# Attention transfers of a batch pair issued at four places in place of one, on one Trainium2 core

## The chip, the cores and the metric

The kernel runs on 1 core of one Trainium2 chip. The metric is the device time of one execution in microseconds (us); a time quoted for a kernel is the median of 3 runs. For the kernel before it is 909.63 us (909.2 to 911.69).

## What is computed

A transformer block on x of 32 batches x 64 tokens x 1024 features in float32:

```python
x = x + attn(cond(x, lengths, ...), Wq, Wk, Wv, Wo)   # cond: a masked long convolution over the 1024 features
x = x + ffn(cond2(x, weights, condition), W_base, gate_W, A, B)  # cond2: a 64x64 channel mix per batch; ffn: linear + top-2 LoRA experts
```

`attn` has 32 query heads of 32 features and 8 key/value heads, rotary positions, a causal mask and a softmax over 64 keys, then the output projection with `Wo`. Its result is added to x (the residual); that sum is called x1 below.

## The kernel before

Five instruction streams are written by hand, one for each engine, and they meet by semaphores only. Four stages follow each other: the convolution; the projections to queries, keys and values (with rotary positions); attention; and the FFN. Products of float32 accuracy are made of three passes over a high and a low part of each operand.

**Between the stages.** The projection stage writes queries, keys and values to DRAM (`q_dram`, `k_dram`, `v_dram`, shown in the profile as q_rows, k_rows, v_rows). Attention works on 16 pairs of batches (`NPAIR`), i = 0 to 15; a unit u = 2i + b is one batch of a pair, 32 units in all. For each pair these transfers are issued on SyncE's queue (SP) by `attention_transfers` (L1002):

- `load_q` (L985): 512 KB of queries of a pair into one of 2 buffers. It waits for `pe_s`, which counts the units whose scores TensorE has finished, so that the buffer is free.
- `load_kv` (L973): 128 KB of keys into one of 2 buffers and four times 64 KB of values into one of 4 buffers; it waits for `pe_s` and `pe_o`.
- `store_x1` (L993): the finished x1 of a pair to DRAM, 512 KB. It waits for `g_x1`, which counts the halves (512 features each) that GpSimd has added: 2 for a pair.
- `load_residual` (L997): 512 KB of x for a later pair, into one of 3 buffers.
- `load_w4` (L1225): one of 8 tiles of the FFN weights, 548 KB, tiles 0 to 3 during attention.

Pairs 0 to 3 are loaded in the stage before; pairs 4 to 15 by `attention_transfers`, in its iterations i = 1 to 12, each for pair i + 3.

**The steps of TensorE in attention** (`attention_matmuls`, L1105) run over w = 2 to 33. Step w does, in this order: `values` of unit w (L1057); `scores` of unit w + 3 (L1037), which waits for `ld_q` and `ld_k` of that unit's pair; and `project` (L1101), the half n = w % 2 of the output projection of pair w // 2 - 1. So step 2i + 2 projects the first half of pair i, and step 2i + 3 begins with values of unit 2i + 3, then scores of unit 2i + 6, the first unit of pair i + 3, and then projects the second half of pair i.

**The other engines.** ScalarE copies the projection out of PSUM (`take_projection`, L1198). GpSimd runs in each of its steps w (`attention_scale`, L1178): `subtract_max` of unit w + 2 (L1128, counted by `g_sub`), `normalise` of unit w + 1 (L1142), and `add_residual` (L1176, counted by `g_x1`), which waits for ScalarE's copy. The half n = 0 of pair i is added in GpSimd's step 2i + 3; with it `g_x1` reaches 2i + 1. VectorE scales the scores (L1119), takes maxima and sums (L1124, L1136 to L1138) and transposes the probabilities (L1148).

Of the kernel before, what the change touches and what calls it, by code (L numbers as in the profile page):

```python
# [22 lines left out]
NPAIR = NB // 2  # L23
NE, RANK = 8, 8
NPROJ = NE + NE * RANK
NBASE = NPROJ + L
# [71 lines left out]
def build(nc, x_conv, x_nat, lens, cond, modes, d_skip,  # L98
          w_qk, w_v, w_o, w_cond, w_ffn, w_b, consts, out):
    ctx = ExitStack()  # L100
    with ctx:
# [3 lines left out]
        def signal(name):  # L105
            return ctx.enter_context(nc.semaphore(name))

        def signals(name, ring):
            return [signal(f"{name}{i}") for i in range(ring)]
# [69 lines left out]
        def take(stack, name, shape, dt=F32):  # L179
            used.setdefault(stack, []).append(int(np.prod(shape[1:])))  # L180
            return sb(name, shape, dt, stack)
# [25 lines left out]
        def spare(name, part, j, shape):  # L207
# [33 lines left out]
        WB_FREE = 4  # L241
# [11 lines left out]
        wb_raw = [take(s5, f"wb_raw_{t}", [P, 2, NBASE]) for t in range(WB_FREE)]  # L253
# [14 lines left out]
        ld_w4, ld_p4 = signals("ld_w4", NJ), signal("ld_p4")  # L268
# [19 lines left out]
        pe_s, v_sc, v_max, g_sub, a_exp, v_sum, v_rec, g_prob = [signal(n) for n in (  # L288
            "pe_s", "v_sc", "v_max", "g_sub", "a_exp", "v_sum", "v_rec", "g_prob")]
        v_pt, pe_o, a_othi, v_otlo, pe_y, a_pr, g_x1 = [signal(n) for n in (  # L290
            "v_pt", "pe_o", "a_othi", "v_otlo", "pe_y", "a_pr", "g_x1")]
# [681 lines left out]
        def load_kv(sp, i):  # L973
            if i >= 2:
                sp.wait_ge(pe_s, 2 * (i - 2) + 2)
            if i >= VR:
                sp.wait_ge(pe_o, 2 * (i - VR) + 2)
            sp.dma_start(kc[:, i % 2, :, :], k_dram[:, :, i * P:(i + 1) * P].rearrange("t p k -> p t k")).then_inc(ld_k[i % 2], 16)
            for quad in range(4):
                G = quad // 2  # L980
                keys = v_dram[G, :, i * P:(i + 1) * P].rearrange("(g k) c -> k g c", g=4)
                sp.dma_start(vc[quad * HB:(quad + 1) * HB, i % VR, :, :, :].rearrange("p g a d -> p g (a d)"),
                             keys).then_inc(ld_v[i % VR], 16)

        def load_q(sp, i):  # L985
            if i >= 2:
                sp.wait_ge(pe_s, 2 * (i - 2) + 2)
            sp.dma_start(q_sb[i % 2][:], q_dram[2 * i:2 * i + 2].rearrange("b p t s -> p b t s")).then_inc(ld_q[i % 2], 16)
# [4 lines left out]
        def store_x1(sp, i):  # L993
            sp.wait_ge(g_x1, 2 * i + 2)
            sp.dma_start(x1_dram[i * P:(i + 1) * P, :], xr[i % 3][:]).then_inc(st_x1[i % 3], 16)

        def load_residual(sp, i):  # L997
            if i >= 3:
                sp.wait_ge(st_x1[(i - 3) % 3], 16 * ((i - 3) // 3 + 1))
            sp.dma_start(xr[i % 3][:], x_nat[i * P:(i + 1) * P, :]).then_inc(ld_x[i % 3], 16)  # L1000

        def attention_transfers(sp):  # L1002
            for i in range(NPAIR):
                if 1 <= i < NPAIR - 3:
                    load_kv(sp, i + 3)
                    load_q(sp, i + 3)
                if i in (6, 8, 10, 12):
                    load_w4(sp, (i - 6) // 2)
                if i == NPAIR - 1:
                    load_x1(sp, 0)  # L1010
                    load_x1(sp, 1)
                    sp.wait_ge(pe_o, NUNIT)
                    for t in range(WB_FREE, WB_EARLY):
                        load_w4(sp, t)
                if i >= 1:
                    store_x1(sp, i - 1)
                    if i + 1 < NPAIR:
                        load_residual(sp, i + 1)
            sp.wait_ge(pe_y, 2 * NPAIR - 1)
            load_w4(sp, 6)  # L1020
            sp.wait_ge(st_x1[(NPAIR - 2) % 3], 16 * ((NPAIR - 2) // 3 + 1))
            load_w4(sp, 7)
            store_x1(sp, NPAIR - 1)
# [176 lines left out]
        def attention_hi(act):  # L1200
            for w in STEPS:
                if w > FIRST:
                    take_projection(act, (w - 1) // 2 - 1, (w - 1) % 2)
                if w < NUNIT:
                    o_hi(act, w)
                if w + 2 < NUNIT:
                    exponentials(act, w + 2)
                for t in W4_TILES.get(w, ()):
                    w4_hi(act, t)
                if w == NUNIT:  # L1210
                    xf_hi(act, 0)
            take_projection(act, NPAIR - 1, 1)

        def load_x1(sp, i):
            if i >= 4:
                sp.wait_ge(st_out[(i - 4) % 4], 16 * ((i - 4) // 4 + 1))
            if i >= NPAIR - 3:
                sp.wait_ge(st_x1[i % 3], 16 * (i // 3 + 1))
            sp.dma_start(x1[i % 4][:], x1_dram[i * P:(i + 1) * P, :]).then_inc(ld_x1[i % 4], 16)

        def w4_place(t, part):

            return part if t < WB_EARLY else 1 - part

        def load_w4(sp, t):  # L1225
            sp.dma_start(wb_raw[t][:, w4_place(t, 1), :], w_ffn[:, t, :]).then_inc(ld_w4[t], 16)

        def ffn_transfers(sp):
            sp.wait_ge(pe_y, 2 * NPAIR)
# [111 lines left out]
                act.activation(xf_batch(i, 0, b), mixed(b), ACT.Copy).then_inc(a_xfhi, 1)  # L1341

        def w4_hi(act, t):
            act.wait_ge(ld_w4[t], 16)
            act.activation(wb[t][:, w4_place(t, 0), :], wb_raw[t][:, w4_place(t, 1), :], ACT.Copy).then_inc(a_w4, 1)

        def w4_lo(v, t):
# [4 lines left out]
        def ffn_hi(act):  # L1352
            act.wait_ge(pe_y, 2 * NPAIR)
            for t in range(WB_EARLY, NJ):
                w4_hi(act, t)
            act.wait_ge(ld_p4, 16 * 2)
            act.activation(bexp_hi[:], bexp_raw[:], ACT.Copy).then_inc(a_p4, 1)
            for i in range(NPAIR + 1):
                if i >= 1:
                    act.wait_ge(v_gate, GATE_STEPS * (i - 1) + 2)  # L1360
                    act.activation(gt[:, 0, :], joint_bank(i - 1, 0)[:, 0:NE], ACT.Exp, bias=gs[:, 1:2],
                                               accum_out=gs[:, 2:3]).then_inc(a_gate, 1)
                    if i > 0:
                        act.wait_ge(pe_ht, i)
                    if 3 * (i - 1) > 0:
                        act.wait_ge(pe_out, 3 * (i - 1))
                    act.activation(ht[:], turned_h(i - 1), ACT.Copy).then_inc(a_hthi, 1)
                if i + 1 < NPAIR:
                    xf_hi(act, i + 1)
# [78 lines left out]
        @block.sync  # L1448
        def _(sp):
            load_parameters(sp)  # L1450
            conv_loads(sp)
            qkv_transfers(sp)
            attention_transfers(sp)
            ffn_transfers(sp)
# [80 lines left out]
```

## Time and profile before

| | before |
|---|---|
| median of 3 runs | 909.63 us (909.2 to 911.69) |
| the profiled execution's own time | 913.52 us |
| its span, first to last instruction | 911.4 us |
| TensorE (PE) busy | 880.3 us, 97% |
| VectorE / ScalarE / GpSimd busy | 444.2 / 202.4 / 395.4 us |
| mean granted TensorE clock | 0.999 |
| DMA | 105.35 MB, mean 116 GB/s |

The rows below come from this one execution. A timeline row gives start, duration, engine, source line, operation, output<-input, shape and count, and in brackets the idle time of that engine just before with what ended it. SPq is SyncE's queue: the duration there is that of issuing a transfer, not of the transfer. A clock of 1.00 is 2.4 GHz, 0.50 is 1.2 GHz. Source lines are those of the kernel before.

### The profile page before, as it was taken

What the parts mean: (1) busy time and instruction counts of PE and PEld (TensorE: products, weight loads), DVE (VectorE), ACT (ScalarE), POOL (GpSimd) and SP (SyncE); (2) the same over time, 40 slices, a digit from 0 to 9 for tenths busy, and PEclk for the clock granted to TensorE, in tenths of its full rate; (3) what the DMA queues carried; (4) which work ended last, traced back from release to release, by engine and by line L of the source; (5) the groups of instructions that cost most, each with busy time, mean ns of one, the idle gap of its engine ahead of it and who ended that gap; (6) DMA issues with size and microseconds to landing.
All of it is one profiled execution on the core that took longest, in us unless ns stands there. A gap on an engine that the chain in (4) does not pass through costs nothing.

```text
span 911.4 us, 24899 instructions
## 1 busy us (share of the span) xinstructions
PE 880.3 (97%) x11054; PEld 766.0 (84%) x11054; DVE 444.2 (49%) x931; ACT 202.4 (22%) x365; POOL 395.4 (43%) x294
## 2 busy tenths in 40 slices
PE   2999999999999999999999999999999999999997
PEld 2888899988888888888777777777789999999997
DVE  6656562111222222259887767788533443334444
ACT  4435652100000000023122222233321101011010
POOL 1344465302555556569978878777511000000000
PEclk9999999999999999999999999999999999999999
DMA  2797787311223222256545464543352121222201
GB/s 68 181 212 198 182 192 184 99 58 58 81 70 103 72 69 74 54 174 171 148 137 158 129 169 149 173 140 108 127 179 88 57 93 57 85 72 69 92 26 69
DMA packets 82090, 105.35 MB, mean 116 GB/s; under 512 B 41536, under 2 KB 54464, under 8 KB 81984
## 3 DMA queue, kind: packets, MB, share of 16 engines
q1 hardware_dynamic: 81472, 103.24, 39.7%
q8 instruction: 87, 1.43, 0.7%
q0 software_dynamic: 512, 0.53, 0.2%
q14 instruction: 19, 0.16, 0.1%
HBM read 74.08 MB, written 29.65 MB: 114 GB/s over the span
## 4 chain that ended last, share of the span: by engine, by line
PE 90%; DMA 5%; DVE 2%; SPq 1%; issue 1%; ACT 0%; DVEq 0%
PE ps L835 24%; PE ps L1287 21%; PE ps L1101 20%; PE ps L541 7%; PE ps L799 5%; PE ps L552 3%; PE ps L1057 3%; PE ps L1037 3%; DMA kpad<-ksb 2%; PE ps L1260 2%; DMA xc<-in_dram 1%; PE ps L1307 1%; DMA toep<-kpad 1%; PE ps L1308 1%; SPq L512 1%
## 5 line engine op out<-in xcount | busy, mean ns | idle before, releaser
L1287 PE MATMUL ps<-wb,xf 128*128 128x420 f32 (+1 forms) x1152 | 195.2, 329 | 0.0
L1287 PEld LDWEIGHTS ps<-wb,xf 128*128 128x128 f32 x1152 | 189.5, 188 | 2.9 <-issue 0.2
L835 PE MATMUL ps<-y_hi,w_hi 128*128 128x512 f32 x320 | 125.1, 391 | 0.0
L835 PE MATMUL ps<-y_hi,w_lo 128*128 128x512 f32 x320 | 124.5, 389 | 0.0
L835 PE MATMUL ps<-y_lo,w_hi 128*128 128x512 f32 x320 | 124.5, 389 | 0.0
L1101 PE MATMUL ps<-y_hi 128*128 128x512 f32 x256 | 103.1, 403 | 0.2
L541 PE MATMUL ps<-xc,toep 64*128 64x192 f32 (+4 forms) x1088 | 97.7, 330 | 4.3 <-DMA xc<-in_dram 2.9
L1101 PE MATMUL ps<-y_hi,y_lo 128*128 128x512 f32 x256 | 100.2, 392 | 1.2 <-issue 1.2
L1101 PE MATMUL ps<-y_lo,y_hi 128*128 128x512 f32 x256 | 100.1, 391 | 0.0
L541 PEld LDWEIGHTS ps<-xc,toep 64*128 64x128 f32 x1088 | 89.9, 187 | 8.3 <-DMA xc<-in_dram 3.3
L942 POOL TENSOR_TENSOR rot<-rot,cst 128x512 f32<-128x512 f32 x40 | 52.7, 1318 | 72.8 <-DVE rot L913 72.8
L1142 POOL TENSOR_TENSOR sc<-sc,stat 128x1024 f32<-128x1024 f32 x32 | 65.7, 2052 | 33.3 <-DVE stat L1138 33.3
L835 PEld LDWEIGHTS ps<-y_hi,w_hi 128*128 128x128 f32 x320 | 60.1, 188 | 12.6
L835 PEld LDWEIGHTS ps<-y_hi,w_lo 128*128 128x128 f32 x320 | 60.1, 188 | 12.6
L835 PEld LDWEIGHTS ps<-y_lo,w_hi 128*128 128x128 f32 x320 | 60.1, 188 | 12.3
L913 DVE LOAD_MASK_SELECT rot<-ps x40 | 0.6, 14 | 141.0 <-PE ps L835 141.0
L1128 POOL TENSOR_TENSOR sc<-sc,stat 128x1024 f32<-128x1024 f32 x32 | 61.2, 1912 | 9.4 <-DVE stat L1124 8.9
L664 POOL TENSOR_TENSOR y_lo<-ym,y_hi 128x256 fp32r<-128x256 f32 x32 | 29.8, 931 | 78.7 <-ACT y_hi L655 78.6
L1119 DVE SCALAR_TENSOR_TENSOR sc<-ps,causal 128x1024 f32<-128x1024 f32 x32 | 39.1, 1223 | 41.3 <-PE ps L1037 41.2
L1101 PEld LDWEIGHTS ps<-y_hi 128*128 128x128 f32 x256 | 48.0, 188 | 12.7 <-issue 1.2
L1101 PEld LDWEIGHTS ps<-y_hi,y_lo 128*128 128x128 f32 x256 | 48.0, 188 | 11.8 <-issue 1.7
L625 DVE TENSOR_TENSOR ym<-ps,valid 128x512 f32<-128x512 f32 x32 | 22.1, 690 | 73.2 <-PE ps L552 55.2
(149 smaller groups left out, 1294.7 us busy)
## 6 DMA issues: line engine op xcount, KB each, us to landing
toep<-kpad SPq DMA_DIRECT2D x62, 272.0 KB, 4.8
xc<-in_dram SPq DMA_DIRECT2D x32, 256.0 KB, 5.6
q_rows<-rf SPq DMA_DIRECT2D x32, 256.0 KB, 2.6
q<-q_rows SPq DMA_DIRECT2D x16, 512.0 KB
xr<-in_dram SPq DMA_DIRECT2D x16, 512.0 KB, 4.6
x_scratch<-xr SPq DMA_DIRECT2D x16, 512.0 KB, 3.0
x<-x_scratch SPq DMA_DIRECT2D x16, 512.0 KB, 3.6
out_dram<-x SPq DMA_DIRECT2D x15, 512.0 KB, 2.6
```

Source lines behind the costliest of these rows:

```text
L541: mm = pe.matmul(ps[:, 2 * (n % 3) + r, first * NB:end * NB], toep[rows, n % TR, at:at + P], xc[rows, n // XH % XR, 1 - c, n % XH, (first ...
L552: mm = pe.matmul(ps[half * HALF:(half + 1) * HALF, 2 * (n % 3) + r, d * NB:NJ * NB], toep[rows, n % TR, at:at + HALF], xc[rows, n // XH % ...
L664: gp.tensor_tensor(y_pair(1, n, 0), ym_pair(n, 0), y_pair(0, n, 0).bitcast(F32), ALU.subtract)
L799: mm = pe.matmul(out, wv[a][:, j, h * P:(h + 1) * P], y[b][:, j, b0:b1, s0:s1], start=(j == 0 and a + b == 0), stop=(j == NJ - 1 and a == 1))
L835: mm = pe.matmul(kq_bank(n), w[a][:, j, :], yt[b][:, j, g * 512:(g + 1) * 512], start=(j == 0 and a + b == 0), stop=(j == NJ - 1 and a == 1))
L942: gp.tensor_tensor(r, r, across(C("sin"), 8), ALU.mult).then_inc(g_rsin, 1)
L1037: mm = pe.matmul(ps[G * S:(G + 1) * S, g, rep * S:(rep + 1) * S], q_sb[i % 2][rows, b, G * REP + rep, :], kc[rows, i % 2, G, b * S:(b + 1) ...
L1101: mm = pe.matmul(ps[:, 6 + n, :], heads, wo(c, t)[:, n, :], start=(at == 0), stop=(at == 3 * NQT - 1))
L1119: v.scalar_tensor_tensor(sc[:, u % CR, :].rearrange("p (g k) -> p g k", g=4), ps[:, 0:4, 0:256], INV_SQRT, across(causal[:].rearrange("p r ...
L1128: gp.tensor_tensor(sc_groups(u), sc_groups(u), along(stat[:, u % CR, 0, :], S), ALU.subtract).then_inc(g_sub, 1)
L1142: gp.tensor_tensor(sc_groups(u), sc_groups(u), along(stat[:, u % CR, 2, :], S), ALU.mult).then_inc(g_prob, 1)
L1287: mm = pe.matmul(joint_bank(i, piece)[:, 0:hi - lo], xf[i % 2][:, a, t, :], wb[t][:, w4_place(t, c), lo:hi], start=(t == 0 and a + c == 0) ...
```

## The change

In iteration i of `attention_transfers` the order and the waits are new. Before, keys and values and then queries of pair i + 3 stand first, then an FFN weight tile (at i = 6, 8, 10, 12), then the store of x1 of pair i - 1 and the residual of pair i + 1. Now the store stands first; the residual follows once `g_sub` reaches 2i + 4; queries of pair i + 3 follow once `g_x1` reaches 2i + 1; keys and values once `g_sub` reaches 2i + 5; and then half a weight tile (at i = 4 to 11). Every tile of the FFN weights, tiles 4 to 7 too, is now loaded by two transfers of half its columns, and ScalarE's `w4_hi` waits for both.

```diff
         def attention_transfers(sp):
             for i in range(NPAIR):
-                if 1 <= i < NPAIR - 3:
-                    load_kv(sp, i + 3)
-                    load_q(sp, i + 3)
-                if i in (6, 8, 10, 12):
-                    load_w4(sp, (i - 6) // 2)
                 if i == NPAIR - 1:
                     load_x1(sp, 0)
                     load_x1(sp, 1)
...
                 if i >= 1:
                     store_x1(sp, i - 1)
                     if i + 1 < NPAIR:
+                        sp.wait_ge(g_sub, 2 * i + 4)
                         load_residual(sp, i + 1)
+                    if i < NPAIR - 3:
+                        sp.wait_ge(g_x1, 2 * i + 1)
+                        load_q(sp, i + 3)
+                        sp.wait_ge(g_sub, 2 * i + 5)
+                        load_kv(sp, i + 3)
+                    if 4 <= i < 4 + 2 * WB_FREE:
+                        load_w4(sp, (i - 4) // 2, (W4_HALVES[(i - 4) % 2],))
...
-        def load_w4(sp, t):
-            sp.dma_start(wb_raw[t][:, w4_place(t, 1), :], w_ffn[:, t, :]).then_inc(ld_w4[t], 16)
+        W4_HALVES = (slice(0, NBASE // 2), slice(NBASE // 2, NBASE))
+
+        def load_w4(sp, t, halves=W4_HALVES):
+            for cols in halves:
+                sp.dma_start(wb_raw[t][:, w4_place(t, 1), cols], w_ffn[:, t, cols]).then_inc(ld_w4[t], 16)
...
         def w4_hi(act, t):
-            act.wait_ge(ld_w4[t], 16)
+            act.wait_ge(ld_w4[t], 16 * 2)
```

**SyncE's queue at the start of attention, iterations 1 and 2** (kc, vc, q: the buffers of keys, values, queries; x_scratch<-xr is the store of x1, xr<-in_dram the residual; a row's bracket names the semaphores it waits for). Before:

```order
L978 DMA kc<-k_rows 128x2x128 [waits pe_s,st_stg2,pe_o,st_stg1,st_stg0]
L982 DMA vc<-v_rows 32x4x128 x4
L988 DMA q<-q_rows 128x2x512 [waits pe_s]
L995 DMA x_scratch<-xr 128x1024 [waits g_x1]
L1000 DMA xr<-in_dram 128x1024
L978 DMA kc<-k_rows 128x2x128 [waits pe_o,pe_s]
L982 DMA vc<-v_rows 32x4x128 x4
L988 DMA q<-q_rows 128x2x512 [waits pe_s]
```

The same two iterations in the changed kernel:

```order
L995 DMA x_scratch<-xr 128x1024 [waits st_stg2,g_x1,st_stg1,st_stg0]
L1000 DMA xr<-in_dram 128x1024 [waits g_sub]
L988 DMA q<-q_rows 128x2x512 [waits pe_s,g_x1]
L978 DMA kc<-k_rows 128x2x128 [waits pe_o,pe_s,g_sub]
L982 DMA vc<-v_rows 32x4x128 x4
L995 DMA x_scratch<-xr 128x1024 [waits g_x1]
L1000 DMA xr<-in_dram 128x1024 [waits st_x10,g_sub]
L988 DMA q<-q_rows 128x2x512 [waits pe_s,g_x1]
```

The queries of pair 4 stood ahead of the first store and waited for `pe_s` alone; they now stand behind the store and the residual and wait for `g_x1` as well. The keys stand behind the queries.

**TensorE at step 3 of attention** (L1040 is `scores` and L1060 `values` in the changed kernel; nothing is moved on TensorE, and the rows read alike before but for the line numbers), the scores of unit 6:

```order
L1060 MATMUL ps<-pt,vc 32x128 [waits a_othi,v_sc,v_otlo,v_pt,ld_v1]
L1060 MATMUL ps<-pt,vc 32x128 x23
L1040 MATMUL ps<-kc,q 64x64 [waits v_sc,ld_k1,ld_q1]
L1040 MATMUL ps<-kc,q 64x64 x31
```

The first score matmul of a unit waits for the query and key transfers of its pair, and the projection of that step stands behind it. This order is unchanged; when those transfers are issued is what the change moves.

## Rows read from the trace of the kernel before

**Rows 1.** Page, part 1: busy us, share of the span, instructions.
```profile
PE 880.3 (97%) x11054; PEld 766.0 (84%) x11054; DVE 444.2 (49%) x931; ACT 202.4 (22%) x365; POOL 395.4 (43%) x294
```

**Rows 2.** Page, part 4: the chain that ended last, share by engine.
```profile
PE 90%; DMA 5%; DVE 2%; SPq 1%; issue 1%; ACT 0%; DVEq 0%
```

**Rows 3.** That chain in order of time, projections of two steps: start, us, what.
```profile
564.73 5.68 PE ps L1101 x24
572.11 5.68 PE ps L1101 x24
```

**Rows 4.** SyncE's queue, waits in 445 to 680 us: total us, times, longest.
```profile
SPq L995 <- POOL xr L1176: 163.1, 16, 15.4
```

**Rows 5.** Timeline of steps 18 and 19 (i = 8), chosen rows.
```profile
563.82 0.91 PE L1037 MATMUL ps<-kc,q 32*64 32x64 f32 x64
...
565.00 1.31 POOL L1176 TENSOR_TENSOR xr<-pr,xr 128x512 f32<-128x512 f32 x1
...
566.33 0.33 SPq L995 DMA_DIRECT2D x_scratch<-xr  x1
...
567.24 0.74 SPq L978 DMA_DIRECT2D kc<-k_rows  x1
...
570.04 0.43 SPq L988 DMA_DIRECT2D q<-q_rows  x1
...
570.34 0.94 PE L1057 MATMUL ps<-pt,vc 32*32 32x128 f32 x48
570.44 0.60 ACT L1198 ACTIVATE pr<-ps 128x512 f32<-128x512 f32 x1 [2.76 <-PE ps L1101]
570.52 1.91 POOL L1142 TENSOR_TENSOR sc<-sc,stat 128x1024 f32<-128x1024 f32 x1 [1.16 <-DVE stat L1138]
...
571.20 0.91 PE L1037 MATMUL ps<-kc,q 32*64 32x64 f32 x64
...
572.39 1.31 POOL L1176 TENSOR_TENSOR xr<-pr,xr 128x512 f32<-128x512 f32 x1
```

**Rows 6.** Page, part 6: transfers, count, KB each, median us from issue to landing.
```profile
x_scratch<-xr SPq DMA_DIRECT2D x16, 512.0 KB, 3.0
x<-x_scratch SPq DMA_DIRECT2D x16, 512.0 KB, 3.6
```

**Rows 7.** The same for 445 to 640 us: queries (no landing shown), keys, weights.
```profile
q<-q_rows SPq DMA_DIRECT2D x12, 512.0 KB
...
wb_raw<-in_dram SPq DMA_DIRECT2D x4, 548.0 KB, 6.2
kc<-k_rows SPq DMA_DIRECT2D x12, 128.0 KB, 4.8
```

**Rows 8.** The same for single key loads, issued at 451.83 us and at 567.24 us.
```profile
kc<-k_rows SPq DMA_DIRECT2D x1, 128.0 KB, 3.2
...
kc<-k_rows SPq DMA_DIRECT2D x1, 128.0 KB, 5.1
```

**Rows 9.** Windows: busy us (count) by engine, granted TensorE clock, DMA share, GB/s.
```profile
567.00:574.50 7.50, 7.50 (x139) 5.86 (x138) 5.72 (x8) 2.32 (x5) 6.18 (x5) 1.00 0.93 269
```

**Rows 10.** First matmul in the timeline; weight loads of L589 in 18:21 and 22.5:24.6 us.
```profile
17.05 1.22 PE L459 MATMUL ps<-ph 128*128 128x128 f32 x4 [17.05 <-DVE ph L450]
...
L589 PEld LDWEIGHTS ps<-cst 128*128 128x128 f32 x8 | 2.6, 336 | 0.5
...
L589 PEld LDWEIGHTS ps<-cst 128*128 128x128 f32 x6 | 1.1, 190 | 0.2
```

**Rows 11.** Windows at the end of the kernel; columns as in rows 9.
```profile
907.50:908.00 0.50, 0.14 (x1) 0.00 (x0) 0.50 (x2) 0.00 (x0) 0.00 (x0) 1.00 0.00 0
...
909.00:909.50 0.50, 0.00 (x0) 0.00 (x0) 0.00 (x0) 0.00 (x0) 0.00 (x0) 1.00 0.99 363
909.50:910.00 0.50, 0.00 (x0) 0.00 (x0) 0.00 (x0) 0.00 (x0) 0.00 (x0) 0.71 0.88 329
910.00:910.50 0.50, 0.00 (x0) 0.00 (x0) 0.00 (x0) 0.00 (x0) 0.00 (x0) 0.50 0.00 0
```

**Rows 12.** Timeline of TensorE: matmuls that an idle time of type "issue" stands before.
```profile
528.19 0.50 PE L1101 MATMUL ps<-y_hi,y_lo 128*128 128x512 f32 x1 [1.25 <-issue]
632.28 0.34 PE L1037 MATMUL ps<-kc,q 32*64 32x64 f32 x7 [0.84 <-issue]
```

**Rows 13.** Copies of FFN weights on ScalarE: duration min/median/max, first and last start.
```profile
L1345 ACT ACTIVATE wb<-wb_raw x8: 1114/1121/1132, 597.1 to 679.1; 128x1096 fp32r<-128x1096 f32 x8
```

## Prediction

> **What bounds the kernel now.** I read the page's busy times first: TensorE is busy 97% of the span, and the next engine 49% [rows 1]. Then the chain that ended last: 90% of it is TensorE [rows 2]. In attention the chain, in order of time, is a train of equal steps: one projection of 5.68 us begins 7.38 us after the last [rows 3], and the 1.7 us between are the values and the scores of the next unit. No step there waits for a transfer. So a transfer that comes earlier gains nothing, and one that comes after its first reader has need of it pushes everything behind it. SyncE's queue has time to spare: it waits 163.1 us for GpSimd's residual add ahead of the 16 stores of x1 [rows 4]. The question is thus one of due times: does each moved transfer still land before TensorE asks for it? I answer it in the timeline of one pair [rows 5], iteration i = 8, where unit 22 is the first of pair 11.
>
> **The queries and keys of pair i + 3.** TensorE asks for them at the scores of unit 2i + 6, at 571.20 us for i = 8 [rows 5]. Before, SyncE issued that pair's transfers one iteration earlier, ahead of the preceding store: what it issues at 567.24 and 570.04 us in the rows shown is already pair 12. The transfers of pair 11 had about a whole pair's time, 14.8 us, to land.
>
> Now they wait for `g_x1` to reach 2i + 1 = 17, the add of the first half of pair 8. That add cannot come before the projection of that half is done, and this projection is the last thing TensorE does in the step before the scores in question. The rows give the chain: the projection ends about 570.4; ScalarE copies it from 570.44 to 571.04; GpSimd is in `normalise` from 570.52 to 572.43, which it starts when VectorE's reciprocal is done; the add stands behind it in GpSimd's order and runs from 572.39 to 573.70 [rows 5]. So the queries are issued at about 573.72 (the store at 566.33 followed its add's end, 566.31, by 0.02 us), which is 2.5 us after TensorE wanted them on chip. The new waits on `g_sub` cost nothing: the subtraction of unit 2i + 4 (count 2i + 5) stands ahead of two adds that SyncE has by then waited for.
>
> **How late.** Issue of the queries takes 0.43 us, so the keys are issued at about 574.2 [rows 5]. The trace shows no landing for the queries. Bounds: a 512 KB transfer alone on the rings took 3.0 us (a store) and 3.6 us (a load) [rows 6]; the keys took 3.2 us where nothing stood ahead, and 5.1 us behind a store and a residual, 1 MB [rows 8], 4.8 in the median [rows 7]. Queries: 573.7 + 3.0 to 3.6 = 576.7 to 577.3. Keys: 574.2 + 3.2 to 5.1 = 577.4 to 579.3. Scores need both. Behind the queries, half of that megabyte, I take the keys halfway between alone and the median, 4.0 us: 578.2. The rings are otherwise empty by then: the store and residual issued at 566 are 1 MB, 4 us at the 269 GB/s that this stretch moved [rows 9]. So TensorE stands still from 571.2 to 578.2: **7.0 us**, with 5.5 (576.7, a query load as fast as the store, keys with it) and 8.1 (579.3) as ends.
>
> Nothing takes this up again. While TensorE waits, VectorE's next scaling waits for the same scores, and ScalarE and GpSimd wait for VectorE. The next step's chain is released by its own scores, so relative to TensorE the add of the next pair's first half comes just as late. It happens once in each of the iterations 1 to 12, the 12 query loads of the stage [rows 7]. Waits: 12 x 7.0 = 84 us.
>
> The Trainium skill speaks against the change here: "DMA: Bandwidth & Descriptors", Rules for kernel authors, advises to issue a transfer early, compute, and wait on its semaphore late. Its section Anatomy of one DMA gives about 2.0 us and the bytes over 436 GB/s for a transfer on GpSimd's path; by an estimate from it the queries would take 3.2 us, the wait would be 5.7 us, and the time 1005.6 us with the clock's term below. The sum stays with the rows' own 3.6 and 4.0.
>
> **The clock after each wait.** The one fall of the clock that the trace shows is at the end: the last matmul ends at 907.6, the granted clock is 1.00 until after 909.5 and 0.50 from 910.0 on [rows 11], level 1.2 GHz. Seven us of idle time are well past those two. What a return costs is seen at the start: after 17.05 us of idle time the first matmul begins at 17.05; weight loads of one shape took 336 ns until 21 and 190 ns from 22.5 us on [rows 10]. So some 4.0 to 5.5 us pass at half speed, and 2.0 to 2.7 us are lost. I take **2.3 us** for each wait, in the projection that follows it: 12 x 2.3 = 27.6 us. Lower end: nothing, if the clock holds.
>
> By the Trainium skill, "TensorE: Matmul & The Clock Gate", Loop structure matters more than you think, a "long DMA wait between every matmul → PE goes cold"; the end of this trace agrees with it (0.50 from 910.0 on). Without it the sum would be rival A's.
>
> **The rest costs nothing.** The store and the residual keep their place after the second add of pair i - 1; the residual's pair is not added until a pair's time later. The values land behind the keys but are read three steps later. The half weight tiles are 8 issues in place of 4 in iterations 4 to 11, and tiles 4 to 7 have 4 more; one issue is below 0.5 us, as the query's is [rows 5], on a queue with 163 us of waiting [rows 4]. Tile 0 is complete after iteration 5, before its first reader, ScalarE's copy at 597.1 us [rows 13], earlier than now, and a tile lands in 6.2 us [rows 7]. If that cover were gone, ScalarE would wait, not TensorE. What the spreading can give back are the gaps that the profile calls issue, 1.25 and 0.84 us [rows 12], should they come from crowded transfers: at most 2.1 us, taken as nothing.
>
> **The sum.** 84 + 27.6 = 111.6 us. On the profiled execution's own 913.5 us this makes 1025.1; that execution was 3.9 us above the median of the runs, so the median forecast is 909.6 + 111.6 = **1021 us**.
>
> **Rivals.**
> A. The clock holds through the waits. For it: after its first matmul TensorE never idles this long in the trace, and the only fall comes after its last. Against: 910.0 [rows 11]. Then 909.6 + 84 = 994 us.
> B. The wait is shorter: the transfers land as fast as the fastest row, and GpSimd is not held up by `normalise`. Copy and add alone would end at 571.04 + 1.31 = 572.35, and 3.0 us later the scores would start: 4.2 us of wait. With the clock's 2.3 us, 78 us: 988. Against: `normalise` is released by VectorE's reciprocal, which follows that step's scores and not the wait.
> C. The other side: the transfers are in time, and only the smoother use of the rings is left. It needs the add of a first half to end before 571.2 - 3.6 = 567.6, or the scores of unit 2i + 6 to stand a step later. The rows show 573.70, 6 us past this point, and TensorE's order stands as it was. If so, the issue gaps would go: 909.6 - 2.1 = 907.5 us, faster by 0.23%; or nothing would change.
> D. The keys come last in the crowd (5.1 us), and the clock costs 2.7 us: 12 x 10.8 = 129.6, 1039 us.
>
> **How the numbers follow.** The forecast has 0.63, A 0.16, B 0.08, D 0.10, C 0.03. The range reaches from the shortest wait of the bounds with no loss of clock, 909.6 + 12 x 5.5 = 975.6, to D, 1039. That takes in A, B and D; some 2 in 10 are left out, for C, for waits that differ from pair to pair and for sizes beyond the nearest rows. A difference under 0.3%, 2.7 us, cannot be told from none here. Slower by more than that is every case but C: 0.97; C gives 0.02 for no change and 0.01 for faster.
>
> **What would show it.** In the profile after: idle time of TensorE ahead of the score matmuls, 12 times near 7 us, ended by the key or query transfer; SyncE's query issue waiting for GpSimd's add; the pair's period up from 14.8 to about 24 us in pairs 1 to 12; the granted clock below 1.00 in that stretch alone; the other stages as long as now. The prediction is wrong if score matmuls start without such waits, if their idle times are below 5 us, or if the clock stays at 1.00.

## The result and the profile after

| | before | changed |
|---|---|---|
| median of 6 runs | 911.03 us (909.2 to 912.96) | 1019.33 us (1015.92 to 1020.9) |
| the profiled execution's own time | 913.52 us | 1020.9 us |
| its span | 911.4 us | 1018.8 us |
| TensorE busy | 880.3 us | 905.5 us |
| TensorE idle (span less busy) | 31.1 us | 113.3 us |
| mean granted clock | 0.999 | 0.945 |

The ratio is 1.1179 (95% interval 1.1158 to 1.12): 108 us slower. The forecast was 1021 us. Source lines are from here on those of the kernel that is spoken of: in the changed kernel `scores` is L1040, `project` L1104, `values` L1060, the residual add L1179, `normalise` L1145 and its copy L1201.

The page after, parts 1, 2 (the granted clock in 40 slices) and 4, which answer to [rows 1, 2]:

```profile
PE 905.5 (89%) x11054; PEld 785.4 (77%) x11054; DVE 444.8 (44%) x931; ACT 202.5 (20%) x365; POOL 395.3 (39%) x294
...
PEclk9999999999999999997777778788899999999999
...
PE 76%; DMA 7%; POOL 7%; DVE 6%; issue 3%; SPq 1%; ACT 0%; DVEq 0%; POOLq 0%
```

TensorE does the same instructions and is busy for 25.2 us longer; its share of the chain has gone from 90% to 76%, and GpSimd, VectorE and the transfers now stand in it. The clock is low in slices 19 to 29 alone, which is attention.

The waits of TensorE on the one hand, of SyncE's queue in 445 to 800 us on the other (engine, line, what it waited for: total us, times, longest):

```profile
PE ps L1040 <- DMA q<-q_rows: 87.7, 12, 8.2
```
```profile
SPq L988 <- POOL xr L1179: 88.6, 12, 8.7
```

There are 12 waits of 7.3 us in the mean, each at the first score matmul of a pair. The issue of the queries waits 12 times for the residual add, as the diff has it. The first of the twelve in the timeline, the counterpart of [rows 5]:

```profile
462.07 0.94 PE L1060 MATMUL ps<-pt,vc 32*32 32x128 f32 x48
462.29 0.26 DVE L1141 RECIPROCAL stat<-stat 128x16 f32<-128x16 f32 x1
462.63 1.90 POOL L1145 TENSOR_TENSOR sc<-sc,stat 128x1024 f32<-128x1024 f32 x1 [1.30 <-DVE stat L1141]
464.49 1.26 POOL L1179 TENSOR_TENSOR xr<-pr,xr 128x512 f32<-128x512 f32 x1
465.78 0.37 SPq L988 DMA_DIRECT2D q<-q_rows  x1
466.25 0.40 SPq L978 DMA_DIRECT2D kc<-k_rows  x1
...
470.28 1.28 PE L1040 MATMUL ps<-kc,q 32*64 32x64 f32 x64 [7.28 <-DMA q<-q_rows]
```

Read it from the end. The scores start at 470.28 after 7.28 us of idle time. The queries were issued at 465.78, 0.03 us after the add's end, and the add stood behind `normalise`, which VectorE's reciprocal released. Values ended at 463.0, so the issue came 2.8 us after the scores were due. In the next eight waits it came 2.4 us after, in the last three 3.3. The transfers of that stretch (445 to 740 us: KB each, median us to landing), for [rows 7]:

```profile
q<-q_rows SPq DMA_DIRECT2D x12, 512.0 KB, 3.9
...
kc<-k_rows SPq DMA_DIRECT2D x12, 128.0 KB, 4.1
```

The clock through that wait and behind it (columns as in [rows 9]: the third number from the end is the granted clock):

```profile
465.00:466.00 1.00, 0.00 (x0) 0.00 (x0) 0.00 (x0) 0.00 (x0) 0.75 (x1) 1.00 0.00 0
466.00:467.00 1.00, 0.00 (x0) 0.00 (x0) 0.00 (x0) 0.00 (x0) 0.00 (x0) 0.62 0.05 18
...
475.00:476.00 1.00, 1.00 (x4) 0.74 (x3) 1.00 (x2) 0.00 (x0) 1.00 (x1) 0.50 0.00 0
476.00:477.00 1.00, 1.00 (x5) 0.82 (x4) 0.99 (x1) 0.00 (x0) 0.06 (x1) 0.76 0.00 0
477.00:478.00 1.00, 1.00 (x6) 0.81 (x5) 0.25 (x1) 0.00 (x0) 0.65 (x1) 1.00 0.00 0
```

It falls to 0.50 (1.2 GHz) some 3.2 us into the idle time and is back at about 476.5, 6 us after the matmuls have begun again. In the first two us behind each of the 12 waits it is 0.50. The projection of that step shows the price, in the chain by time: 7.99 us, and 7.37 two pairs later, where a projection at the full clock took 5.68 [rows 3].

```profile
471.56 7.99 PE ps L1104 x24
...
520.67 7.37 PE ps L1104 x24
```

The FFN stage has kept its length. Windows of 233 us from its start to the end, first after, then before: the busy times agree to 0.5 us.

```profile
786.00:1019.00 233.00, 228.26 (x2219) 220.07 (x2217) 95.28 (x368) 29.08 (x81) 3.39 (x2) 1.00 0.21 73
```
```profile
679.00:912.00 233.00, 227.86 (x2216) 219.68 (x2214) 95.25 (x368) 28.66 (x81) 2.98 (x2) 1.00 0.21 73
```

So the 107.4 us between the two profiled executions are 87.7 us of waits and 25.2 us of longer matmuls, less 5.5 us: TensorE's other idle time is 25.6 us in place of 31.1. Of these 5.5 us, 3.4 lie ahead of the first wait, in the stages before attention, and 2.1 behind it. The latter is the size of the two gaps of [rows 12], 1.25 and 0.84 us, and this trace has neither.

### The profile page after: what moved, and what is told of

Same layout as the page of the kernel before. It is cut to its first block, busy times and chain, and to the rows that moved or that the text cites. A ratio compares the mean times of both kernels' runs of the same rounds, so it can differ in the third digit from the quotient of the medians.

```text
span 1018.8 us, 24933 instructions
## 1 busy us (share of the span) xinstructions
PE 905.5 (89%) x11054; PEld 785.4 (77%) x11054; DVE 444.8 (44%) x931; ACT 202.5 (20%) x365; POOL 395.3 (39%) x294
## 4 chain that ended last, share of the span: by engine, by line
PE 76%; DMA 7%; POOL 7%; DVE 6%; issue 3%; SPq 1%; ACT 0%; DVEq 0%; POOLq 0%
PE ps L835 21%; PE ps L1293 19%; PE ps L1104 12%; PE ps L541 7%; DMA q<-q_rows 5%; PE ps L799 4%; PE ps L552 3%; PE ps L1040 3%; POOL sc L1145 3%; POOL sc L1131 2%; PE ps L1266 2%; DVE sc L1122 2%; PE ps L1060 2%; DVE stat L1127 2%; POOL xr L1179 1%
## 5 line engine op out<-in xcount | busy, mean ns | idle before, releaser
L1104 PE MATMUL ps<-y_hi 128*128 128x512 f32 x256 | 112.5, 440 | 0.2 <-POOL y_lo L970 0.2
L1040 PE MATMUL ps<-kc,q 32*64 32x64 f32 x2048 | 33.6, 264 | 87.7 <-DMA q<-q_rows 87.7
L1104 PE MATMUL ps<-y_lo,y_hi 128*128 128x512 f32 x256 | 108.3, 423 | 0.0
L1104 PE MATMUL ps<-y_hi,y_lo 128*128 128x512 f32 x256 | 106.8, 417 | 0.0
L1131 POOL TENSOR_TENSOR sc<-sc,stat 128x1024 f32<-128x1024 f32 x32 | 61.0, 1907 | 113.3 <-DVE stat L1127 113.2
L1040 PEld LDWEIGHTS ps<-kc,q 32*64 32x64 f32 x2048 | 28.9, 159 | 95.0 <-DMA q<-q_rows 90.6
L1145 POOL TENSOR_TENSOR sc<-sc,stat 128x1024 f32<-128x1024 f32 x32 | 65.6, 2051 | 35.4 <-DVE stat L1141 35.4
L1104 PEld LDWEIGHTS ps<-y_hi 128*128 128x128 f32 x256 | 53.5, 209 | 14.8 <-issue 0.8
L1104 PEld LDWEIGHTS ps<-y_hi,y_lo 128*128 128x128 f32 x256 | 53.1, 207 | 12.3
```

Source lines behind the costliest of these rows:

```text
L1040: mm = pe.matmul(ps[G * S:(G + 1) * S, g, rep * S:(rep + 1) * S], q_sb[i % 2][rows, b, G * REP + rep, :], kc[rows, i % 2, G, b * S:(b + 1) ...
L1104: mm = pe.matmul(ps[:, 6 + n, :], heads, wo(c, t)[:, n, :], start=(at == 0), stop=(at == 3 * NQT - 1))
L1131: gp.tensor_tensor(sc_groups(u), sc_groups(u), along(stat[:, u % CR, 0, :], S), ALU.subtract).then_inc(g_sub, 1)
L1145: gp.tensor_tensor(sc_groups(u), sc_groups(u), along(stat[:, u % CR, 2, :], S), ALU.mult).then_inc(g_prob, 1)
```

## Experiments

The theory: everything that is lost comes from queries and keys that are issued after TensorE is due to read them, first as idle time and then as lost clock. Rivals: the new order or the other moves cost by themselves; the 20 us beyond the waits are not the clock. Runs were timed beside the kernel before on the same chip, whose medians were 912.58 us beside runs 1, 3, 4 and 5 and 911.76 us beside runs 2, 6, 7 and 8; differences below are against these.

**1. The early loads back, the rest of the change kept.**

```diff
             for i in range(NPAIR):
+                if 1 <= i < NPAIR - 3:
+                    load_kv(sp, i + 3)
+                    load_q(sp, i + 3)
...
-                    if i < NPAIR - 3:
-                        sp.wait_ge(g_x1, 2 * i + 1)
-                        load_q(sp, i + 3)
-                        sp.wait_ge(g_sub, 2 * i + 5)
-                        load_kv(sp, i + 3)
```

> Of the change this leaves the store ahead of the residual with its new wait, and the FFN weights in halves; keys, values and queries stand again at the head of the iteration, without a wait for the residual add. Theory (the whole loss is queries and keys that are issued after TensorE is due to read them): 909 to 913 us, no idle time of TensorE ahead of the score matmuls, clock 1.00. Rival (part of the loss is the other moves: the residual's wait, 8 more issues on SyncE's queue, half transfers): more than 915 us.

Measured: 913.14 us, ratio 1.0011 (0.9988 to 1.0034), clock 0.999. No wait of TensorE for queries or keys is left in the profile; ahead of one score matmul it calls 0.5 us issue, as it does 0.84 us before [rows 12]. The residual's wait, the halves of the weights and the further issues cost nothing that can be measured; all of the loss is in the five lines taken out.

**2. The same places, one pair ahead.**

```diff
-                    if i < NPAIR - 3:
-                        sp.wait_ge(g_x1, 2 * i + 1)
-                        load_q(sp, i + 3)
-                        sp.wait_ge(g_sub, 2 * i + 5)
-                        load_kv(sp, i + 3)
...
+                if i < NPAIR - 4:
+                    sp.wait_ge(g_x1, 2 * i + 1)
+                    load_q(sp, i + 4)
+                    sp.wait_ge(g_sub, 2 * i + 5)
+                    load_kv(sp, i + 4)
```

> The changed kernel with the same four places and the same new waits, but the queries, keys and values that are issued there are those of pair i + 4 instead of i + 3, so that each has a pair's time to land. Theory: no idle time ahead of the scores, the time of the kernel before within 0.3%; what the even spacing can give back on top are the issue gaps, at most 2 us. Rival (the waits or the spacing cost something by themselves, on SyncE's queue or the rings): over 0.5% slower.

Measured: 912.03 us, ratio 1.0005 (0.9991 to 1.002). With all four places and every new wait in force, the loss is gone as soon as the loads belong to the next pair; their two query and key buffers are free at that point already. And the even spacing that the change has in it gains nothing that can be measured: transfers were hidden before, and two gaps like those of [rows 12] are there still, 1.0 and 0.6 us. This is the repaired form of the change, and it does not beat the kernel before.

**3. Without the wait for the add.**

```diff
                     if i < NPAIR - 3:
-                        sp.wait_ge(g_x1, 2 * i + 1)
                         load_q(sp, i + 3)
```

> The changed kernel without the one wait of SyncE for the add of a pair's first half; the order of the transfers stays. Theory: queries and keys are then issued some 6.5 us earlier, at once behind the store and the residual, and land 1.0 to 2.5 us after the scores are due instead of 7.3; such idle times are too short for the clock to fall: 12 x 1.0 to 2.5, 921 to 940 us. Rival (the new order behind the store and residual is what costs, not the wait): near 1019 us, idle times near 7 us as in the changed kernel.

Measured: 957.77 us, ratio 1.048 (1.0441 to 1.0519). The idle times are about as expected, 1.7 to 2.7 us; the time is not. Waits of TensorE, one of the waits, and the windows around it:

```profile
PE ps L1039 <- DMA q<-q_rows: 24.9, 11, 2.7
```
```profile
563.52 1.12 PE L1039 MATMUL ps<-kc,q 32*64 32x64 f32 x45 [2.44 <-DMA q<-q_rows]
```
```profile
562.00:563.00 1.00, 0.00 (x0) 0.00 (x0) 0.00 (x0) 0.00 (x0) 1.00 (x2) 1.00 0.95 216
563.00:564.00 1.00, 0.48 (x33) 0.51 (x35) 0.00 (x0) 0.00 (x0) 0.85 (x2) 0.55 0.38 85
...
569.00:570.00 1.00, 1.00 (x4) 0.72 (x3) 1.00 (x2) 0.00 (x0) 1.00 (x1) 0.54 0.00 0
570.00:571.00 1.00, 1.00 (x6) 0.82 (x5) 1.00 (x1) 0.00 (x0) 0.08 (x1) 1.00 0.00 0
```

The clock fell here after 2 us of idle time and stayed at 0.50 for some 6.8 us, most of them beside matmuls. It fell behind 10 of the 12 waits, in five of them only after the scores had begun. TensorE is busy 902.8 us, 22.5 more than in the kernel before, nearly as much more as in the changed kernel. So of the 50 us that this execution lost (962.87 us, the slowest of the four) 27.5 are waits, and the rest is the clock; that such waits are too short for it was wrong. The end of the kernel before had hinted at it [rows 11]: there the clock fell 2.1 us after the last matmul.

**4. The wait filled with matmuls that nobody reads.**

```diff
             values(pe, u)
+            if u % 2 == 1 and 5 <= u <= 27:
+                keep_busy(pe, 14)
```

> The changed kernel with 14 matmuls that nobody reads in each of the 12 waits (6.0 us at the full clock), ahead of the score matmuls. Theory (beyond the waits of 87.7 us, the remaining 20 us are the clock's fall to 1.2 GHz in each wait): the granted clock stays at 1.00, about 1.2 us of idle time are left ahead of the scores, the scores start when they did, and the time is 999 us (996 to 1003). Rival (the 20 us are transfers beside the projection, or engines that have to start up again): 1019 us.

Measured: 999.93 us, clock 0.996. The waits that are left, in the same view as for the changed kernel:

```profile
PE ps L1040 <- DMA q<-q_rows: 13.6, 12, 1.7
```

They are 1.1 us each, beside 6 us of filling. From the end of the values to the scores the 12 waits, filling included, are 88.5 us, so the scores start about as late as in the changed kernel (87.7); yet the time is 87 us above before and not 108, and work without use has won 21 us. The clock fell twice all the same in the profiled execution, once ahead of the first wait and once behind the last. The price of the waits and that of the clock are thus apart.

**5. Only the queries late.** Keys and values are loaded at the head of the iteration, as before.

```diff
             for i in range(NPAIR):
+                if 1 <= i < NPAIR - 3:
+                    load_kv(sp, i + 3)
...
                         load_q(sp, i + 3)
-                        sp.wait_ge(g_sub, 2 * i + 5)
-                        load_kv(sp, i + 3)
```

> Of the three loads only the queries wait for the add; keys and values are early as before. Theory: the queries alone hold the scores until they land, 3.9 us after their issue, 0.4 to 0.6 us before the keys did: waits of about 6.8 us, 1012 us (1008 to 1016). Rival (the queries land last in the changed kernel, as the profile's releaser reads): no difference to 1019 us. Rival (only the keys matter): 911 us.

Measured: 1019.86 us, ratio 1.1165 (1.113 to 1.1201): no clear difference to the changed kernel, against the theory by the time alone. The waits are shorter as the theory has it, 79.3 us in place of 87.7, 6.6 us each. The chain by time shows why, here and then for the changed kernel:

```profile
473.63 4.22 DMA q<-q_rows
477.85 0.04 issue
477.90 1.29 PE ps L1040 x61
```
```profile
465.78 3.86 DMA q<-q_rows
469.64 0.64 issue
470.28 1.28 PE ps L1040 x59
```

With the keys on chip, the scores start 0.04 us after the queries land. In the changed kernel they start 0.64 us after, without a visible reason: that is the keys, which land 3.9 us after their issue at 466.25, at 470.15. Why the time does not show it can be read in two parts. TensorE is busy 912.8 us, 7.3 more than in the changed kernel. From the start of the first wait to the end (first here, then the changed kernel; length, then TensorE's busy time):

```profile
470.89:1022.80 551.91, 468.13 (x5768) 406.94 (x5768) 244.72 (x554) 95.25 (x197) 154.27 (x97) 0.89 0.27 88
```
```profile
463.00:1018.80 555.80, 463.54 (x5769) 403.99 (x5768) 244.77 (x554) 95.30 (x197) 154.40 (x97) 0.90 0.28 88
```

Of the 8.4 us that the waits are shorter, 4.6 are lost again in longer matmuls at the low clock and 3.9 are kept. These 3.9 are hidden in the profiled execution by the stages ahead of the first wait, which took 470.9 us in place of 463.0: TensorE idled 5.2 us longer there, and its clock was 0.86 in 50 to 75 us, in the convolution. The other three executions have no profile, so how much of it they share is open.

**6. Only the queries late, and the wait filled** with 14 matmuls as in 4.

> The kernel whose queries alone wait for the add, with the same 14 matmuls in each wait as in the run that kept TensorE busy in the changed kernel. Theory (the shorter wait, 6.6 us in place of 7.3, was lost again to a longer time at the low clock): with the clock held, 12 x 0.7 = 8 us less than that run, 79 us above the kernel before (75 to 83). Rival (the keys' landing is of no account): the same as that run, 87 us above it.

Measured: 988.4 us, 76.6 above before, ratio 1.0839 (1.0807 to 1.0871), against 87.4 above before and 1.0949 (1.0913 to 1.0986) in 4. With the clock held (1.0), the keys' later landing is worth 11 us by the medians. By the waits, filling included, it is 9.5 us: 79.0 us in place of the 88.5 of 4, 0.8 us a pair; the two falls of the clock in 4 are in the difference of the times too. So the theory stands, and 5 hid it, in part behind the clock. Why the clock stayed low for longer in 5 than in the changed kernel is not settled.

**7. Only keys and values late.** The queries are loaded at the head of the iteration.

```diff
             for i in range(NPAIR):
+                if 1 <= i < NPAIR - 3:
+                    load_q(sp, i + 3)
...
                         sp.wait_ge(g_x1, 2 * i + 1)
-                        load_q(sp, i + 3)
                         sp.wait_ge(g_sub, 2 * i + 5)
```

> Only keys and values wait for the add; the queries are early as before. Theory: the keys alone hold the scores; issued 0.47 us earlier than in the changed kernel, with nothing ahead of them, they land 3.2 to 3.9 us after the issue: 12 idle times of 6.0 to 6.7 us, and a loss of clock of 1.7 to 2.7 us each: 92 to 113 us above the kernel before. Rival (only the queries matter, as the profile's releaser reads): the time of the kernel before.

Measured: 991.83 us, 80 above before, ratio 1.0873 (1.0847 to 1.09). The keys alone hold the scores, so the rival is out; but the time is below the 92 to 113 us that were expected:

```profile
PE ps L1041 <- issue: 59.9, 12, 5.6
```
```profile
kc<-k_rows SPq DMA_DIRECT2D x12, 128.0 KB, 2.2
```

With nothing ahead of them the keys land in 2.2 us, where the one load of [rows 8] took 3.2; why that one was slower is open. The 12 waits are 5.0 us each, and TensorE is busy 21.6 us longer than before, so the clock's share is much as expected and the waits are short of it. The profile calls them issue: in these runs it names the queries or nothing as the releaser of this matmul, and never the keys, also where they alone were late.

**8. Without the wait for the add, and the rest of the wait filled** with 5 matmuls.

> The kernel without the wait for the add, with 5 matmuls that nobody reads (2.1 us at the full clock) in each of the 12 waits. Theory (its 45 us are waits of 2.3 us and a fall of the clock after each): the clock stays at 1.00, the scores start as late as there, and 12 x 2.3 = 28 us are left above the kernel before (24 to 32). Rival (the rest is something else than the clock): 45 us above it as without the filling.

Measured: 949.11 us, 37 above before, ratio 1.0395 (1.0366 to 1.0424): between theory and rival, and outside the 24 to 32 that were expected. The clock held (0.999), but the waits grew, since the store and with it the queries were issued later than in 3, relative to TensorE. First the step in 3 (values start at 573.25), then the same step here (values start at 565.43):

```profile
573.36 0.60 ACT L1200 ACTIVATE pr<-ps 128x512 f32<-128x512 f32 x1 [4.83 <-PE ps L1103]
574.03 1.27 POOL L1178 TENSOR_TENSOR xr<-pr,xr 128x512 f32<-128x512 f32 x1 [0.76 <-ACT pr L1200]
...
575.33 0.34 SPq L995 DMA_DIRECT2D x_scratch<-xr  x1
```
```profile
565.63 1.91 POOL L1146 TENSOR_TENSOR sc<-sc,stat 128x1024 f32<-128x1024 f32 x1 [1.29 <-DVE stat L1142]
...
567.49 1.29 POOL L1180 TENSOR_TENSOR xr<-pr,xr 128x512 f32<-128x512 f32 x1
...
568.81 0.34 SPq L995 DMA_DIRECT2D x_scratch<-xr  x1
```

In 3 the projection ran at the low clock, GpSimd was done with `normalise` before it ended, and the store went out 2.08 us after the values began. Here the projection is quick, `normalise` stands ahead of the add again, and the store goes out at 3.38 us. So it is in 7 of the 12 pairs; in the other five the store of run 3 was late as well (3.1 to 3.5 us). From the end of the values to the scores the 12 waits, filling included, are 35.6 us here and 27.5 in 3. The 8 us between them give back over a third of the clock's 22.5 us; the 37 us that are left above before are little more than the waits.

## Why the prediction was right

- **What bounds.** TensorE, and no transfer on the chain. Right: where the loads were in time, any spacing gave the same time (runs 1 and 2).
- **The due time.** Queries issued 2.5 us after the scores are due; measured 2.8 in the first wait, 2.4 in the next eight and 3.3 in the last three (i = 10 to 12, see below), 2.7 in the mean. The chain of copy, `normalise`, add and issue is the one in the rows.
- **How late.** 7.0 us foretold, 7.3 measured; 84 us, and 87.7. The keys were taken to land last, 4.0 us after issue; they landed after 3.9 to 4.3. Run 6 shows that they do land last, by some 0.8 us. That 4.0 came so close is in part luck: it was the middle between two rows, and of these the 3.2 us for keys alone is 2.2 in run 7. The queries took 3.9 us, outside the 3.0 to 3.6 that were allowed for them; the sum did not feel it, since the keys land later still. The 3.2 us estimated for the queries from the Trainium skill's figure for a transfer on GpSimd's path ("DMA: Bandwidth & Descriptors", Anatomy of one DMA) were short of the 3.9 measured on SyncE's queue.
- **The clock.** 2.3 us for each wait foretold; 25.2 / 12 = 2.1 measured, 1.7 of it in the projections behind the waits (the 12 take 6.61 to 8.08 us, 7.41 in the mean) and 0.4 in the scores (1.28 us in place of 0.91). Rival A, a clock that holds, is out: the clock was 0.50 behind every wait, and run 4 shows A's time, 87 us above before, when the clock is mostly made to hold. The Trainium skill ("TensorE: Matmul & The Clock Gate", Loop structure matters more than you think) has TensorE go cold when a long wait for a transfer stands between matmuls; this trace agrees, with 0.50 behind each of the 12 waits.
- **The rest.** Nothing foretold, nothing measured: 1.0011 with the loads early. The other side, rival C, is what run 2 made true by hand, and even then there was no gain. Rival D is out by the keys' 3.9 to 4.3 us and the clock's 2.1.
- **The sum.** 111.6 us foretold, 108.3 by the medians and 107.4 between the profiled executions: the waits took 3.7 us more than foretold, the clock 2.4 less, and 5.5 us of other idle time were not there in this execution. So the terms hold to a tenth; that the time itself came within 2 us is luck, as their errors cancel in part, and so does that of the starting point (909.6 us forecast from, 911.03 measured beside the change).

Rival B (`normalise` out of the way) did not happen in the changed kernel, but its mechanism is real: it is the 1.3 us between the stores of runs 3 and 8.

## What to carry to other kernels

Before moving a transfer behind a wait, place the wait's release and the transfer's first reader on one time line; here the release came from the very step before the reader, and the lateness could be read from the trace of before to 0.3 us in nine waits of twelve. If loads are to be spread, let them run a whole period ahead as their buffers allow; the order itself was free. And a wait on TensorE costs more than its idle time: the lost clock behind it added over a quarter here (25.2 on 87.7 us).

## What was not expected

- **The clock falls after short waits, too.** In run 3 idle times of 1.7 to 2.7 us were followed by 0.50 in 10 cases of 12, and the matmuls took 22.5 us longer, against 25.2 behind waits three times as long. Time that is won by a shorter wait can be lost again in the clock (4.6 of 8.4 us in run 5).
- **`normalise` takes longer beside one of VectorE's operations.** At i = 10 to 12 the waits are 7.8 to 8.2 us instead of 6.9 to 7.3. There `normalise` takes 2.83 us instead of 1.90 on GpSimd, while VectorE subtracts an FFN weight tile, and the queries are issued 3.3 us after the scores are due:

```profile
678.85 1.24 DVE L1355 TENSOR_TENSOR wb<-wb_raw,wb 128x1096 fp32r<-128x1096 f32 x1
679.01 2.83 POOL L1145 TENSOR_TENSOR sc<-sc,stat 128x1024 f32<-128x1024 f32 x1 [1.29 <-DVE stat L1141]
```

The kernel before has the same pair of rows four times, 2.83 us each. That the one slows the other was seen side by side and not tried apart.
